# Key and value diagonals written by DMA from operands split once, context loaded by channel, products on zeros ahead of the first work

## The reference

```
q = layernorm(x) @ Wq + bq          # 16 heads of 32 channels
k, v = ctx @ Wk + bk, ctx @ Wv + bv # 64 keys for each batch
a = softmax(clip(q k^T / sqrt(32), -1e4, 1e4))   # all equal if any is NaN
x = x + (a v) @ Wo + bo
h = layernorm(x) @ W1 + b1          # 2048 channels
phase = cos(theta) * w_re + sin(theta) * w_im
h = h + phase * w_im * sin(theta + 0.1 h) * 0.1
x = x + relu(h) @ W2 + b2
```

## Time and profile before

| | us |
|---|---|
| three timed runs, median (lowest to highest) | 2065.92 (2063.91 to 2067.17) |
| the profiled execution's own time | 2066.23 |
| its span in the profile | 2064.50 |
| TensorE busy in it | 2043.2 (99%) |
| VectorE, ScalarE, GpSimd busy | 1360.5, 1149.5, 1042.6 |

### The profile page before, as it was taken

One profiled execution on the slowest core, in us unless ns is written; L12 is line 12 of the kernel. 1 busy time (PEld: TensorE's weight loads), 2 busy tenths in 40 slices (PEclk: granted clock), 3 DMA queues, 4 the chain that ended last, 5 costly groups with the idle time before them and its releaser, 6 DMA issues.

```text
span 2064.5 us, 27142 instructions
## 1 busy us (share of the span) xinstructions
PE 2043.2 (99%) x9762; PEld 1717.7 (83%) x9762; DVE 1360.5 (66%) x2031; ACT 1149.5 (56%) x2041; POOL 1042.6 (51%) x757
## 2 busy tenths in 40 slices
PE   8899999999999999999999999999999999999999
PEld 6788888888888888888888888888888888888887
DVE  7988888888876765555555555555555556565554
ACT  5667676767664755454454545545455454554543
POOL 4777777777776355334353443534334354343522
PEclk9999999999999999999999999999999999999999
DMA  5122232222213421111212112121111211112100
GB/s 185 57 101 94 88 103 97 78 98 87 72 60 120 119 80 26 57 41 42 63 33 69 42 41 57 36 72 41 42 41 51 72 42 41 42 51 72 41 21 21
DMA packets 133654, 133.93 MB, mean 65 GB/s; under 512 B 68872, under 2 KB 84744, under 8 KB 133520
## 3 DMA queue, kind: packets, MB, share of 16 engines
q1 hardware_dynamic: 132512, 132.16, 21.5%
q10 hardware_dynamic: 1008, 0.04, 0.0%
HBM read 81.83 MB, written 50.35 MB: 64 GB/s over the span
## 4 chain that ended last, share of the span: by engine, by line
PE 92%; DVE 4%; ACT 2%; POOL 1%; issue 1%; DMA 0%; SPq 0%; ACTq 0%; DVEq 0%; POOLq 0%
PE psum L1177 29%; PE psum L1179 29%; PE psum L1178 29%; PE psum L1270 2%; PE psum L1183 1%; DVE hid L1109 1%; POOL prob L614 0%; ACT act_hi L847 0%; DVE act_lo L1112 0%; ACT hid L858 0%; DMA ctx_sb<-in_ctx 0%; POOL prob L609 0%; DVE prob L1030 0%; ACT frac L843 0%; DVE top L1036 0%
## 5 line engine op out<-in xcount | busy, mean ns | idle before, releaser
L666 POOL TENSOR_TENSOR frac<-turns,frac 128x512 f32<-128x512 f32 x256 | 333.6, 1303 | 827.0 <-DVE frac L1137 827.0
L1109 DVE SCALAR_TENSOR_TENSOR hid<-frac,gain,hid 128x512 f32<-128x512 f32 x256 | 323.0, 1262 | 143.3 <-ACT frac L843 142.3
L1177 PE MATMUL psum<-w_hi,act_hi 128*128 128x512 f32 x1024 | 398.4, 389 | 0.8 <-DVE act_lo L1112 0.8
L1179 PE MATMUL psum<-w_hi,act_lo 128*128 128x512 f32 x1024 | 398.3, 389 | 0.0
L1178 PE MATMUL psum<-w_lo,act_hi 128*128 128x512 f32 x1024 | 398.3, 389 | 0.0
L847 ACT ACTIVATE act_hi<-hid 128x512 fp32r<-128x512 f32 x256 | 162.3, 634 | 357.0 <-DVE hid L1109 357.0
L856 ACT ACTIVATE turns<-psum,u_shift 128x512 f32<-128x512 f32 x256 | 176.7, 690 | 324.9 <-PE psum L1179 266.7
L1112 DVE SCALAR_TENSOR_TENSOR act_lo<-hid,act_hi 128x512 fp32r<-128x512 f32 x256 | 197.4, 771 | 179.2 <-ACT act_hi L847 179.2
L1137 DVE TENSOR_SCALAR frac<-turns 128x512 f32<-128x512 f32 x256 | 111.5, 436 | 247.2 <-ACT turns L856 247.2
L1177 PEld LDWEIGHTS psum<-w_hi,act_hi 128*128 128x128 f32 x1024 | 192.1, 188 | 41.0 <-issue 1.2
L1178 PEld LDWEIGHTS psum<-w_lo,act_hi 128*128 128x128 f32 x1024 | 192.2, 188 | 40.0
(11 more groups left out here) (162 smaller groups left out, 4198.5 us busy)
## 6 DMA issues: line engine op xcount, KB each, us to landing
res<-in_x SPq DMA_DIRECT2D x64, 256.0 KB, 2.9
x_dram<-res SPq DMA_DIRECT2D x64, 256.0 KB, 2.0
x_sb<-in_x SPq DMA_DIRECT2D x15, 1024.0 KB, 5.9
x_sb<-x_dram SPq DMA_DIRECT2D x15, 1024.0 KB, 5.6
xn<-turn_dram SPq DMA_DIRECT2D x30, 512.0 KB, 4.9
out<-x_sb SPq DMA_DIRECT2D x15, 1024.0 KB, 4.2
turn_dram<-stage SPq DMA_DIRECT2D x112, 128.0 KB, 2.4
stage<-in_w SPq DMA_DIRECT2D x32, 256.0 KB, 2.9
```

What stands on the lines that cost most here:

```text
L666: pool.tensor_tensor(frac[:, j % 2, :], turns[:, j % 2, :], frac[:, j % 2, :], ALU.subtract)\
L1109: dve.scalar_tensor_tensor(out=hid[:, j % 2, :], in0=frac[:, j % 2, :], scalar=gain[:, f:f + 1], in1=hid[:, j % 2, :], op0=ALU.mult, op1=A ...
L1177: pe.matmul(o, a_hi, b_hi, start=first, stop=False)
L1179: return pe.matmul(o, a_lo, b_hi, start=False, stop=last)
```

## The change

It has five parts.

- **Context by channel.** The host hands the context over transposed; one DMA brings it to `ctxt_sb`, and ScalarE and VectorE split it from there. The 12 transposes are gone. The means are taken at step 5 (`M_STEP`) from `v_sb`, 16 small products in place of 12, and the 12 products at the start are gone with them.
- **Keys split once.** For each group, ScalarE writes the rounded keys of all batches to `kt[:, g % 2, 0]` and VectorE the rest (`keys_to_hi`, `keys_to_lo`). DMAs copy the first batch's 64 columns of each head from `kt` to the zeroed `kbd` (`place_first_keys`), others store `kt` to DRAM (`store_keys`) and write the later batches' places (`place_keys`). The 32 maskings by GpSimd, 32 roundings and 32 subtractions are gone.
- **Values split once,** likewise: ScalarE and GpSimd split `v_sb` to `v_parts` four times (GpSimd 128x512 each), stored to DRAM and placed in `vbd` by `place_values` in pieces of 128 B. Again 32 maskings, roundings and subtractions are gone.
- **Products on zeros.** VectorE zeroes `kbd` (2048 elements a partition) and `vbd` (3072) as its first two instructions; TensorE then multiplies zeros by zeros 30 times before the first tile's transposes and twice after them (`warm`).
- **Phases on GpSimd.** The operations on theta are 22 small ones on GpSimd, after its first `rstd`.

SP's order changes too: the placements, the stores and x's second tile come before Wo's load.

```diff
-CONSTS = 15
-PAR_REDUCED = 13
+CONSTS = 7
+WARM = 30, 2
+PAR_REDUCED = 19
@@ SP
+            def store_keys(g):
+                sp.wait_ge(kt_lo_done, g + 1)
+                sp.dma_start(k_dram[:, g], kt[:, g % 2].bitcast(F32)).then_inc(kt_stored[g], 16)
+
+            def place_first_keys(g):
+                sp.wait_ge(kt_lo_done, g + 1)
+                sp.wait_ge(zeros_done, 1)
+                for h in range(HG):
+                    rows, cols = slice(h * D, (h + 1) * D), slice(h * KEYS, (h + 1) * KEYS)
+                    sp.dma_start(kbd[rows, g, :, cols].bitcast(F32), kt[rows, g % 2, :, 0:KEYS].bitcast(F32))\
+                        .then_inc(kbd_first[g], 16)
+
+            def place_keys(b, pair):
+                groups = slice(2 * pair, 2 * pair + 2)
+                if b == 1:
+                    for g in range(2 * pair, 2 * pair + 2):
+                        sp.wait_ge(kt_stored[g], 16)
+                sp.wait_ge(s_psum, S_BANKS * (b * GB - KC + 2 * pair + 2))
+                for h in range(HG):
+                    rows, cols = slice(h * D, (h + 1) * D), slice(h * KEYS, (h + 1) * KEYS)
+                    sp.dma_start(kbd[rows, groups, :, cols].bitcast(F32),
+                                 k_dram[rows, groups, :, b * KEYS:(b + 1) * KEYS]).then_inc(kbd_in[pair], 16)
...
             sp.dma_start(u_dram, u_sb[:]).then_inc(u_stored, 16)
             for n in range(TILES * NB):
                 t, blk = divmod(n, NB)
+                b = n // GB + 1
+                if b < B:
+                    if n % GB == 0:
+                        place_keys(b, 0)
+                    if n % GB == 2:
+                        place_keys(b, 1)
+                    if n % GB == 3:
+                        place_values(b, 0)
+                    if n % GB == 5:
+                        place_values(b, 1)
                 sp.wait_ge(y_done, n + 1)
@@ GpSimd
-            def mask_keys(b, g):
...
+            def values_to_lo(n):
+                pool.wait_ge(vn_hi_done, n + 1)
+                pool.tensor_tensor(v_parts[:, :, 1, :], by_pair(v_sb[:, n, :]), v_parts[:, :, 0, :].bitcast(F32), ALU.subtract)\
+                    .then_inc(vn_lo_done, 1)
@@ ScalarE
+            def keys_to_hi(g):
                 act.wait_ge(kt_psum, g + 1)
+                if g >= 2:
+                    act.wait_ge(kt_stored[g - 2], 16)
+                    act.wait_ge(kbd_first[g - 2], 16 * HG)
+                act.activation(kt[:, g % 2, 0, :], psum[:, K_BANKS[g], :], ACT.Identity, bias=bk_sb[:, g:g + 1])\
+                    .then_inc(kt_hi_done, 1)
@@ VectorE
+            dve.memset(kbd[:].bitcast(F32), 0.0).then_inc(zeros_done, 1)
+            dve.memset(vbd[:].bitcast(F32), 0.0).then_inc(zeros_done, 1)
             layer_stats(0, range(NB))
...
+            def keys_to_lo(g):
+                dve.wait_ge(kt_hi_done, g + 1)
+                dve.scalar_tensor_tensor(out=kt[:, g % 2, 1, :], in0=psum[:, K_BANKS[g], :], scalar=bk_sb[:, g:g + 1],
+                                         in1=kt[:, g % 2, 0, :].bitcast(F32), op0=ALU.add, op1=ALU.subtract)\
+                    .then_inc(kt_lo_done, 1)
...
+                if i in K_STEPS:
+                    keys_to_lo(K_STEPS.index(i))
                 if i in V_STEPS:
                     values_rows(V_STEPS.index(i))
@@ TensorE
+            def warm(n):
+                for _ in range(n):
+                    pe.matmul(psum[:, WARM_BANK, :], kbd[:, 0, 0, 0:P], kbd[:, 1],
+                              start=True, stop=True)
+            pe.wait_ge(zeros_done, 1)
+            warm(WARM[0])
...
-                    if t % TPB == 0:
-                        pe.wait_ge(kbd_lo_done, (t // TPB) * KC + g + 1)
+                    if t == 0:
+                        pe.wait_ge(kbd_first[g], 16 * HG)
+                    elif t % TPB == 0 and g % 2 == 0:
+                        pe.wait_ge(kbd_in[g // 2], 16 * HG * (t // TPB))
```

More of the change, by code:

```diff
@@ L103 @@
 WO_STEPS = (3, 4, 5, 5)
-MEAN_BANK = 5
+WARM_BANK = 1
 M_BANK = U_BANK = 4
@@ L112, in has_burst, with xattn_ffn @@
     return i % KC == KC - 2 and i + 2 < GROUPS
-def xattn_ffn(nc, x, ctx_768, wq, bq, wk, bk, wv, bv, bv_channels, wo, bo, w1, b1, phases, w_real, w_imag,
-              w2, b2, out, x1_dram, v_dram, u_dram, turn_dram):
+def xattn_ffn(nc, x, ctxt, wq, bq, wk, bk, wv, bv, wo, bo, w1, b1, phases, w_real, w_imag,
+              w2, b2, out, x1_dram, k_dram, v_dram, u_dram, turn_dram):
     x_rows = x.rearrange("b (t n p) c -> (b t) p n c", n=NB, p=P)
@@ L180, in xattn_ffn @@
         q_full = sbuf(pa, "q_full", [P, TOK])
-        v_in = sbuf(pa, "v_in", [P, 2, C])
-        vbd_hi = sbuf(pa, "vbd_hi", [P, KC, PAIRS, P], F32R)
-        vbd_lo = sbuf(pa, "vbd_lo", [P, KC, PAIRS, P], F32R)
+        v_parts = sbuf(pa, "v_parts", [P, 2, 2, 2 * P], F32R)
+        vbd = sbuf(pa, "vbd", [P, 2, 2, 2, 3 * P], F32R)
         prob = sbuf(pa, "prob", [P, SCORE_BUFS, NB * HG, KEYS])
@@ L410, in load_values @@
                 for half in range(2):
-                    sp.dma_start(v_in[half * KEYS:(half + 1) * KEYS, b % 2, :], v_dram[b]).then_inc(v_dma[b % 2], 16)
+                    places = vbd[half * KEYS:(half + 1) * KEYS, pair].bitcast(F32).rearrange("p s g (j c) -> p (s g j) c", j=PAIRS)
+                    cols = slice(half * D, (half + 1) * D)
+                    values = v_dram[b][:, pair].rearrange("k s (q c) -> k (s q) c", c=2 * D)
+                    sp.dma_start(places[:, :, cols], values[:, :, cols]).then_inc(vbd_in[pair], 16)
@@ L617, in _ @@
                     q_to_lo(i + 1)
+                if i - 1 in V_STEPS:
+                    values_to_lo(V_STEPS.index(i - 1))
             pool.wait_ge(nan_count, 1)
@@ L947, in _ @@
                 dve.wait_ge(ctxt_hi_done, k + 1)
[L948 removed]
+                dve.tensor_tensor(ctxt_lo[:, k, :], ctxt_sb[:, k, :], ctxt_hi[:, k, :].bitcast(F32), ALU.subtract)\
                     .then_inc(ctxt_lo_done, 1)
[L951 to L959 removed]
+            def keys_to_lo(g):
[3 more added lines that the diff above has]
+                    .then_inc(kt_lo_done, 1)
             def values_rows(n):
@@ L1043, in _ @@
                                           ALU.subtract).then_inc(pt_lo_done, 1)
-                if next_keys(i):
-                    keys_to_lo(*next_keys(i))
-                if next_values(i):
-                    values_to_lo(*next_values(i))
                 if i < GROUPS:
@@ L1221, in _ @@
                 transposes(0, k, xt_bank(0, k))
-            for n in range(B // 2):
-                for k in range(KK):
-                    m = pe.matmul(psum[:, MEAN_BANK, k * B + 2 * n:k * B + 2 * n + 2],
-                                  ctx_sb[:, n, k * P:(k + 1) * P], pick[:], start=True, stop=True)
-            m.then_inc(ctx_mean_psum, 1)
-            pe.wait_ge(ctxt_lo_done, KK)
-            pe.wait_ge(kv_lo_done, KK)
+            warm(WARM[1])
             keys(0)
@@ L1252, in _ @@
                         m = product(psum[:, half, at * SG:(at + 1) * SG], (q_hi[:, i % 2, toks], q_lo[:, i % 2, toks]),
-                                    (kbd_hi[:, g, :], kbd_lo[:, g, :]))
+                                    (kbd[:, g, 0, :], kbd[:, g, 1, :]))
                         if at == BANK // SG - 1:
@@ L1315, in _ @@
                     pe.wait_ge(q_full_done, i + 1)
+                    pe.wait_ge(vn_done, B // 2)
                     for k in range(KC):
-                        for kk in range(KK):
-                            m = pe.matmul(psum[:, M_BANK, k * B:(k + 1) * B], wv_sb[:, kk, k * P:(k + 1) * P],
-                                          ctx_mean[:, kk, :], start=kk == 0, stop=kk == KK - 1)
+                        for n in range(B // 2):
+                            m = pe.matmul(psum[:, M_BANK, k * B + 2 * n:k * B + 2 * n + 2],
+                                          v_sb[:, n, k * P:(k + 1) * P], pick[:], start=True, stop=True)
                     m.then_inc(vm_psum, 1)
@@ L1357, in _ @@
                         pe.wait_ge(pt_lo_done, PAIRS * late + j + 1)
-                        m = product(psum[:, o_bank(i), :], (vbd_hi[:, lg, j, :], vbd_lo[:, lg, j, :]),
+                        m = product(psum[:, o_bank(i), :], [vbd[:, lg // 2, part, lg % 2, j * P:(j + 1) * P] for part in range(2)],
                                     (pt_hi[:, j, :], pt_lo[:, j, :]), j == 0, j == PAIRS - 1)
```

289 lines of the change are left out of this document (109 added, 180 removed).

## The result

The changed kernel takes 2072.16 us (median of 7 runs, 2068.95 to 2073.46) against 2065.92 before (7 runs). The ratio is 1.0032, 95% interval 1.0020 to 1.0043. So the kernel is slower by 0.2 to 0.3%, 4.5 to 6.2 us. The forecast was 2070.8, slower or no change at nearly even chances. It came near with one half of its argument right: the new wait with its half clock cost what was forecast, by two errors that cancel, and the 2.5 us that were to be won before it were not won.

A forecast was written before the change was run, and what follows sets the result against it. TensorE, 99% busy, was taken as the bound from about step 6, a GpSimd, ScalarE and VectorE loop before it. 2066.23 - 2.5 (before step 8) + 7.1 (step 8) = 2070.8 us, range 2062.5 to 2075.

The forecast's parts named there:

- Step 8: Scores wait for keys placed behind SP's wait for `u_done`: 5.5 us (4.3 to 8.9) plus 1.6 of half clock.
- The start: Memsets delay VectorE 1.25 us, then 18 operations of 0.61 us; step 0's values and scores start 2.4 us earlier.
- The loop: Steps 1 to 6: otherwise unchanged from step 3, `vbd_lo` gone; first `y` of step 6 comes 2.5 us earlier.
- the 0.5 us charged for GpSimd's phases: VectorE operations with two SBUF operands sometimes wait for GpSimd's 22 phase operations: 0.5 us, at most 2.5.
- The mean product: Step 5: 16 products in place of 12 take 0.9 us more, hidden where TensorE waits for VectorE right behind.
- The half clock: In the loop, priced only in the upper bound: 1.6 us regained in each of two stretches at clock 0.91.
- The order of the keys: Step 1: VectorE waits for group 3's keys, written after the normalisations; 1.9 of 3.2 us left at step 2's subtraction.
- The loop gives way: Rival, steps 3 to 6: VectorE no longer late, TensorE's waits and slow clock go; 2063.1 us, chance 0.14.
- Short memsets: Rival, start: memsets at half price, VectorE ready when rows arrive, 1.25 us more gained; 2069.6 us, chance 0.14.
- GpSimd holds VectorE up: Rival, start: 13 VectorE operations each meet a GpSimd one in full, 2.5 us for 0.5; 2072.8 us, chance 0.15.
- The placement isn't late: Rival, step 8: the last row lands before 110 us, so no wait; seen as impossible, no chance given.
- What I called wrong signs: Step 8 starting without a wait, no TensorE waits from 45 to 90 us, or new idling behind 130 us.

The follow-up runs named there:

- e1_place: The changed kernel with the second batch's keys (groups 0 and 1) placed ahead of SP's wait for `u_done`: 2065.47 us, ratio 0.9996 to the kernel before.
- e10_place_keys_vlate: e6_place_keys with GpSimd's low halves of the values behind the next step's halved sums: 2061.02 us, ratio 0.9975 to the kernel before.
- e2_mean_short: The changed kernel with 4 mean products in step 5 in place of 16 (value means wrong): 2068.70 us, ratio 1.0014 to the kernel before.
- e6_place_keys: e1_place with ScalarE writing group 3's keys ahead of step 1's four normalisations: 2062.25 us, ratio 0.9980 to the kernel before.
- e4_mean4: The changed kernel with the mean product in step 4 in place of step 5: 2072.30 us, ratio 1.0031 to the kernel before.
- e12_and_vbd_gpsimd: e10_place_keys_vlate with the zeros of `vbd` written by GpSimd in place of VectorE: 2059.08 us, ratio 0.9969 to the kernel before.
- e3_fill: The changed kernel with unread products added ahead of the waits for `pt_lo` and `q_lo` in steps 4 and 5: 2072.15 us, ratio 1.0032 to before.
- e5_place_mean4: e1_place with the mean product in step 4 in place of step 5: 2064.22 us, ratio 0.9993 to the kernel before.
- e8_place_fill: e1_place with unread products added only at TensorE's waits for `pt_lo` and `q_lo` in steps 3 to 5: 2064.07 us, ratio 0.9996 to before.

## Why the prediction was near, and which step of it failed

**Step 8 was right.** Forecast 5.5 + 1.6 = 7.1 us, measured 4.7 + 2.4 = 7.1. The wait is shorter since the four issues took 0.44 us each, not 0.5, and the placements landed 1.7 to 2.0 us after their issue, not 2.7: they carry 32 KB each, a quarter of those of `v_in`, and this was the lower bound's argument. TensorE ran at half clock for 4.8 us, not the 3.4 of the earlier trace rows (half of those 3.37 is 1.7, too, not 1.6). The two errors cancel, so that the sum of 7.1 was met exactly is luck. e1_place takes the term away and gives back 5.4 to 6.7 us in the medians.

**The start was right.** Memsets at 0.86 ns an element, between the value taken (1.06) and the bound (0.53): 4.4 us in all, not 5.5, but they began 0.4 later and stood 0.6 apart, so they ended at 6.2 for 6.3; VectorE ready 1.0 later, not 1.25; 18 operations from 12.70 to 23.7, the 18 x 0.61 = 11.0 us that had been forecast; 2.6 us won for 2.4.

**The loop failed.** Forecast 2.5 us won at the first `y`, measured 0.75 lost. Up to the scores of step 5 the sum held, by two errors that cancel: TensorE was 2.6 us ahead there. "In steps 3 to 6 the loop stays as it is" overlooked that GpSimd now makes the values' low halves, 1.29 us each, ahead of the halved sums, where it had masks of about 0.7 behind them. So the lead of VectorE's loop grew from 2.1 to 2.3 us, not to 3.0. e10_place_keys_vlate, which moves them, has the total of step 4 1.3 us earlier; its time is 1.2 us less, which the noise doesn't separate from nothing. But the 0.5 us charged for GpSimd's phases wasn't paid. From step 5 on 3.3 us were lost on TensorE in the profiled execution, by two steps of the argument (together 3.6, less the wait of 0.19 that is gone):

- *The mean product was not hidden* (0.75 us). The prediction put its extra 0.9 us into a wait of TensorE "right behind it". That wait was 0.19 us long before, and with TensorE late there was none. e2_mean_short shows that the product counts: 2.1 to 3.5 us less in the medians.
- *The half clock was priced only where it could get better* (2.86 us). I had asked how much of it could come back, not what more of it would cost. From 73.4 to 79.1 us TensorE, not the loop, became the bound of the steps, and the loop's lead of 2.3 us was gone by step 6 (0.7). Why the clock fell there isn't shown, and that it did is known of the two slowest executions only.

Profile to profile, 2066.23 + 0.75 + 7.1 = 2074.1, less 0.3 for a wait ahead of step 9 in the kernel before (118.9 to 119.2 us) that step 8's delay swallows, is near the 2073.46 measured. In these terms, which are those of the forecast's sum, 2070.8 was 2.7 us too low. That it is 1.4 us from the first median and on the second is luck: the profiled execution of before stood 0.31 us above its median, those of the changed kernel 1.30 and 2.45.

**The order of the keys** was forecast (1.9 of 3.2 us left, 2.1 measured), but as a given. e6_place_keys shows that swapping two blocks on ScalarE is worth about 3 us, half clock included.

**The rivals.** *The loop gives way* was half true: e2_mean_short and e4_mean4 have TensorE 4.4 to 4.6 us ahead of before at step 6, once neither the product nor half clock stands in the way. *Short memsets*: the price is between the two, and in e12_and_vbd_gpsimd the scores of step 0 come the 1.1 us earlier that the zeros had cost. *GpSimd holds VectorE up* is refuted: VectorE kept its pace of 0.60 to 0.61 us. It is GpSimd that was held, its operations on 16 elements taking up to 0.81 us in place of 0.25, the reverse of the earlier trace rows. The Trainium skill, "SBUF — State Buffer", section "Who interferes with whom", leaves both open: it has the order of issue, not the kind of operation, decide which of the two is blocked. The trace of before shows the one case and that of the changed kernel the other. *The placement isn't late* is refuted by the wait.

**What I called wrong signs** didn't appear: no idling behind 130 us, and TensorE waits in steps 3 to 5. "The scores of step 7 about 2.5 us earlier" was the sign that failed: they came at 98.64, 0.75 later than before (97.89).

## What to carry to other kernels

When a change puts transfers into a queue, list what each engine's queue makes them stand behind: one placement behind a wait for something else cost more than everything else in the change, and moving one line gave it back. Freed time in a loop is worth only what the next waits leave, so list every operation that the change adds on each engine of the loop, helpers too, and ask of each "hidden" operation how long the wait is that hides it. Its parts in a better order, and one of them on another engine, are 7 us faster than before, so a change that loses is worth taking apart.

## What the runs showed of the hardware

- **Half clock follows the mean product.** Its 32 records of 2 columns take 3.5 us, in which TensorE is counted as busy. In 11 of the 12 profiles that hold it in full (the changed kernel and the experiments), and in the kernel before with 24 records of 8 columns, the granted clock fell to half (1.2 GHz) 2.4 to 4.8 us after it began, whether it began at 67, 75, 79 or 81 us; e4_mean4 is the exception. e2_mean_short, which leaves most of it out, had no fall between 60 and 100 us. The kernel before has a second such case at its start: the context's means, 24 records of 2 columns from 14.28 us, and the clock fell at 16.75. The changed kernel has no means there, and its clock stayed full until 72.4. In e3_fill five products of 512 columns directly behind the mean product didn't prevent the fall (82.6 us); none were put between its records. That the mean product causes the fall isn't shown beyond this: the changed kernel's fall at 72 us has none ahead of it.
- **The same wait, two prices.** In e2_mean_short and e3_fill, after the same wait at step 8 (4.6 us), the granted clock stayed at half for 6.8 and for 3.4 us. With 1.7 us of time for each 3.4, such differences show in single times: the 33 runs of the kernel before beside e5_place_mean4 to e8_place_fill fell into 2063.3 to 2064.2 (9 runs) and 2065.8 to 2067.2 (24 runs), with none between, and the 9 are exactly those with a granted clock of 0.999 over the span, the 24 those with 0.998 or 0.997. Beside the other experiments it is alike, with a few runs up to 2069.57, at 0.998 down to 0.996. So the groups go with the clock; where in the kernel the slower runs lost it no pair of profiles shows.
- **Zeros.** 3072 elements a partition took 2.62 us on VectorE and 2.66 on GpSimd. The Trainium skill, "VectorE: DVE Perf Modes", section "Zero memsets can be issued as uint32 (trn2)", has one cycle per element. That the price per element doesn't depend on the count agrees: 0.86 ns over 2048 elements and 0.85 over 3072. But it is less than the 1.06 ns that an element more costs VectorE's reductions.
